# Reordering the VectorE and ScalarE queues of a graph attention kernel: V's low parts, softmax parts and squares

## The reference

```python
output = einsum('bni,io->bno', x, weight)
q, k   = x @ wq, x @ wk
alpha  = einsum('bno,bmo->bnm', q, k)
alpha  = maximum(alpha, 0.0) * (adj != 0)
alpha  = softmax(alpha, axis=1)
y      = x + einsum('bnm,bmo->bno', alpha, output)
out    = (y - mean(y)) / sqrt(var(y) + 1e-5)
```

## Time and profile before

| | before |
|---|---|
| median of 3 runs | 539.57 us (539.29 to 541.98) |
| the profiled execution, device time | 538.71 us |
| its span, first to last instruction | 536.9 us |
| granted TensorE clock | 0.997 |
| TensorE matmul busy | 515.9 us, 96% |
| VectorE busy | 386.4 us, 72% |
| ScalarE busy | 321.1 us, 60% |
| GpSimd busy | 267.2 us, 50% |
| one group, span 141.90 to 205.50 | 63.60 us, of which TensorE busy 62.13 us |

### The profile page before, as it was taken

One profiled execution on the slowest core, in us unless ns is written; L12 is line 12 of the kernel. 1 busy time (PEld: TensorE's weight loads), 2 busy tenths in 40 slices (PEclk: granted clock), 3 DMA queues, 4 the chain that ended last, 5 costly groups with the idle time before them and its releaser, 6 DMA issues.

```text
span 536.9 us, 9927 instructions
## 1 busy us (share of the span) xinstructions
PE 515.9 (96%) x3259; PEld 466.1 (87%) x3259; DVE 386.4 (72%) x741; ACT 321.1 (60%) x745; POOL 267.2 (50%) x198
## 2 busy tenths in 40 slices
PE   8999999999999999999999999999999999999993
PEld 6889997898979988799978989789897998879993
DVE  4767745779568786588857796577956978656676
ACT  5666565385853856648554676538585385664663
POOL 0397964358525567148551495435852565710002
PEclk9999999999999999999999999999999999999998
DMA  7405231053600625025240344205260062302344
GB/s 268 163 0 197 83 132 43 21 155 120 235 20 20 215 85 208 20 81 185 105 175 20 117 155 160 95 20 183 90 234 20 23 211 104 150 1 74 122 156 156
DMA packets 30719, 62.05 MB, mean 116 GB/s; under 512 B 2032, under 2 KB 3056, under 8 KB 30704
## 3 DMA queue, kind: packets, MB, share of 16 engines
q1 hardware_dynamic: 30704, 61.87, 33.3%
HBM read 45.09 MB, written 16.78 MB: 115 GB/s over the span
## 4 chain that ended last, share of the span: by engine, by line
PE 84%; DVE 9%; issue 3%; ACT 2%; DMA 1%; POOL 0%; DVEq 0%; POOLq 0%; SPq 0%; ACTq 0%
PE o_bank L293 11%; PE o_bank L295 11%; PE o_bank L294 11%; PE chain L293 10%; PE chain L295 9%; PE chain L294 9%; PE bank_y L293 5%; PE bank_y L294 5%; PE bank_y L295 5%; DVE p_lo L1052 3%; DVE v_lo L979 3%; PE bank_z L293 2%; PE bank_z L295 2%; PE bank_z L294 2%; DVE parts L991 1%
## 5 line engine op out<-in xcount | busy, mean ns | idle before, releaser
L1349 POOL TENSOR_TENSOR s_lo<-xs,s_hi 128x512 fp32r<-128x512 f32 x60 | 87.7, 1480 | 49.4 <-ACT s_hi L668 49.0
L1344 POOL TENSOR_TENSOR a_lo<-xt,a_hi 128x512 fp32r<-128x512 f32 x42 | 59.9, 1434 | 46.1 <-ACT a_hi L660 46.1
L1354 POOL TENSOR_TENSOR rstd<-var_eps,minus_half 128x4 f32<-128x4 f32 x15 | 15.3, 1018 | 117.1 <-DVE var_eps L1076 117.1
L295 PE MATMUL o_bank<-t_hi,a_lo 128*128 128x256 f32 x256 | 72.4, 283 | 0.0
L294 PE MATMUL o_bank<-t_lo,a_hi 128*128 128x256 f32 x256 | 72.4, 283 | 0.0
L293 PE MATMUL o_bank<-t_hi,a_hi 128*128 128x256 f32 x256 | 72.4, 283 | 0.0
L1052 DVE SCALAR_TENSOR_TENSOR p_lo<-soft,inv_sum,p_hi 128x256 fp32r<-128x256 f32 x64 | 55.2, 881 | 17.8 <-ACT p_hi L747 17.8
L1340 POOL TENSOR_TENSOR xs<-xt 128x512 f32<-128x512 f32 x30 | 39.6, 1336 | 41.8 <-DMA xt<-in_x_t 23.9
L687 ACT COPY parts<-chain 128x256 f32<-128x256 f32 x90 | 33.3, 371 | 42.6 <-PE chain L295 41.5
L677 ACT COPY parts<-chain 128x512 f32<-128x512 f32 x42 | 24.7, 587 | 47.1 <-DVE v_lo L979 32.0
L293 PE MATMUL o_bank<-v_hi,p_hi 128*128 128x512 f32 (+1 forms) x132 | 50.7, 384 | 1.4 <-DVE soft L1035 1.4
(11 more groups left out here) (191 smaller groups left out, 1599.0 us busy)
## 6 DMA issues: line engine op xcount, KB each, us to landing
xt<-in_x_t SPq DMA_DIRECT2D x64, 256.0 KB, 3.4
xn<-in_x SPq DMA_DIRECT2D x16, 1024.0 KB, 5.3
out<-xn SPq DMA_DIRECT2D x15, 1024.0 KB, 4.3
adj<-in_adj_t SPq DMA_DIRECT2D x16, 512.0 KB, 6.0
xn<-in_w SPq DMA_DIRECT2D x4, 256.0 KB, 4.6
xn<-in_wq_t SPq DMA_DIRECT2D x4, 256.0 KB, 6.0
parts<-in_wk_t SPq DMA_DIRECT2D x4, 256.0 KB, 6.1
out<-xn SPq DMA_DIRECT2D x4, 256.0 KB, 2.0
```

What stands on the lines that cost most here:

```text
L295: return nc.tensor.matmul(dst, a[1], b[0], start=False, stop=last, skip_group_check=shared)
L1344: nc.gpsimd.tensor_tensor(a_lo[:, slot, u], xt[:, u], a_hi[:, slot, u].bitcast(F32), ALU.subtract).then_inc(a_lo_ready[slot], 1)
L1349: nc.gpsimd.tensor_tensor(s_lo[:, slot, s], xs[:, s], s_hi[:, slot, s].bitcast(F32), ALU.subtract).then_inc(s_lo_ready[slot], 1)
```

## The change

All semaphore counts stay as they are; only the order of steps in ScalarE's and VectorE's lists changes. No step is added or removed.

- VectorE, start of a group: v_lo A22, v_lo A21 and p_lo 0 of z go ahead of T's first sum, p_lo 1 ahead of its second.
- ScalarE, start of a group: the first squares of y go from between two casts of V to just before copy_t(P6, 0), split_s(S2) stands ahead of v_hi A21, p_hi 1 and split_s(S4) ahead of copy_t(P1, 0), p_hi 3 ahead of copy_t(P6, 0).
- Both, pair a: each p part goes one or more steps ahead of V's parts; VectorE's p_lo 2 and 3 go ahead of mask(b, 0). ScalarE's casts for the next group's a (split_a, split_s) go behind p_hi 3.
- Last step: the four squares of pair 14 go between V's copies and splits on ScalarE; on VectorE its variance goes ahead of v_lo A12 and its first normalisation ahead of v_lo A21.

```diff
--- before.py
+++ after.py
@@ -762,20 +762,20 @@
                 a, b, z, y = 2 * i, 2 * i + 1, 2 * i - 1, 2 * i - 2
                 split_p(z, 0)
                 split_v(z, A22)
-                centred_squares(y, 0, 0)
+                split_s(i, 1, S2)
                 split_v(z, A21)
+                split_p(z, 1)
+                split_s(i, 1, S4)
                 copy_t(i, P1, 0)
-                split_s(i, 1, S2)
-                split_s(i, 1, S4)
                 copy_t(i, P1, 1)
                 split_s(i, 1, S1)
                 split_a(i, 1, A22)
-                split_p(z, 1)
                 split_p(z, 2)
+                split_p(z, 3)
+                centred_squares(y, 0, 0)
                 copy_t(i, P6, 0)
                 split_t_a(i, A11)
                 copy_t(i, P6, 1)
-                split_p(z, 3)
                 copy_t(i, P5, 0)
                 copy_t(i, P5, 1)
                 centred_squares(y, 0, 1)
@@ -799,30 +799,27 @@
                 exponent(a, 2)
                 copy_v(a, P6, 1)
                 exponent(a, 3)
+                split_p(a, 0)
                 copy_v(a, P5, 0)
                 copy_v(a, P5, 1)
-                split_p(a, 0)
-                if more:
-                    split_a(i + 1, 0, A21)
                 split_p(a, 1)
                 v_released(a)
                 split_v(a, A22)
+                split_p(a, 2)
+                split_v(a, A11)
+                split_p(a, 3)
                 if more:
+                    split_a(i + 1, 0, A21)
                     split_s(i + 1, 0, S2)
+                split_v(a, A12)
+                if more:
                     split_s(i + 1, 0, S3)
                     split_s(i + 1, 0, S1)
-                split_v(a, A11)
-                split_v(a, A12)
-                if more:
                     split_a(i + 1, 0, A11)
-                split_p(a, 2)
+                split_v(a, A21)
                 if more:
                     split_a(i + 1, 0, A12)
                     split_s(i + 1, 0, S4)
-                split_v(a, A21)
-                split_p(a, 3)
-
-                if more:
                     split_a(i + 1, 0, A22)
 
                 act.wait_ge(t_lo_ready, 8 * i + 4 + T_LO[1][A12])
@@ -851,24 +848,24 @@
                 for r in range(R):
                     exponent(p, r)
                 copy_v(p, P1, 0)
+                split_p(p, 0)
                 copy_v(p, P1, 1)
-                split_p(p, 0)
+                split_p(p, 1)
+                split_p(p, 2)
                 copy_v(p, P6, 0)
-                split_p(p, 1)
+                centred_squares(p - 1, 0, 0)
                 copy_v(p, P6, 1)
-                split_p(p, 2)
+                centred_squares(p - 1, 0, 1)
                 copy_v(p, P5, 0)
                 split_p(p, 3)
                 copy_v(p, P5, 1)
-                centred_squares(p - 1, 0, 0)
+                centred_squares(p - 1, 0, 2)
                 v_released(p)
                 split_v(p, A22)
-                centred_squares(p - 1, 0, 1)
+                centred_squares(p - 1, 0, 3)
                 split_v(p, A11)
                 split_v(p, A12)
-                centred_squares(p - 1, 0, 2)
                 split_v(p, A21)
-                centred_squares(p - 1, 0, 3)
                 for r in range(R):
                     centred_squares(p, 1, r, by_tile=True)
 
@@ -1086,13 +1083,13 @@
                 a, b, z, y = 2 * i, 2 * i + 1, 2 * i - 1, 2 * i - 2
                 split_v(z, A11, V_AT[1])
                 sum_v(z, A21)
+                split_v(z, A22, V_AT[1])
+                split_v(z, A21, V_AT[1])
+                split_p(z, 0)
                 sum_t(i, A11, 0)
-                split_v(z, A22, V_AT[1])
-                split_p(z, 0)
+                split_p(z, 1)
                 sum_t(i, A11, 1)
-                split_p(z, 1)
                 split_p(z, 2)
-                split_v(z, A21, V_AT[1])
                 split_p(z, 3)
                 sum_t(i, A22, 0)
                 sum_t(i, A22, 1)
@@ -1124,18 +1121,18 @@
                 split_t_b(i, A22)
                 split_t_b(i, A21)
                 invert(a)
+                split_p(a, 0)
                 sum_v(a, A22)
-                split_p(a, 0)
+                split_p(a, 1)
                 sum_v(a, A11)
                 split_v(a, A22, V_AT[0])
-                split_p(a, 1)
+                split_p(a, 2)
                 split_v(a, A11, V_AT[0])
+                split_p(a, 3)
                 split_v(a, A12, V_AT[0])
                 sum_v(a, A21)
 
                 mask(b, 0)
-                split_p(a, 2)
-                split_p(a, 3)
                 split_v(a, A21, V_AT[0])
                 mask(b, 1)
                 residual(a, i, 0, 0)
@@ -1308,11 +1305,12 @@
             sum_v(last, A11)
             split_v(last, A22, V_LAST)
             split_v(last, A11, V_LAST)
+            variances(last - 1)
             split_v(last, A12, V_LAST)
             sum_v(last, A21)
+            normalise(last - 1, 0, 0)
             split_v(last, A21, V_LAST)
-            variances(last - 1)
-            for r in range(R):
+            for r in range(1, R):
                 normalise(last - 1, 0, r)
             for r in range(R):
                 residual(last, GROUPS - 1, 1, r, bank=bank_y[:, 0] if r == R - 1 else None)
```

## The result

| | before | after |
|---|---|---|
| median | 539.43 us (538.47 to 541.98, 4 runs) | 524.39 us (523.67 to 526.05, 4 runs) |
| span of the profiled execution | 536.9 us | 522.0 us |
| first T matmul of group 1 | 77.62 us | 77.63 us |
| a group, first T matmul to first T matmul | 63.60 to 63.65 us | 61.64 us, all six |
| last residual chain, first residual to end of the last normalisation | 6.55 us | 6.55 us |

A forecast was written before the change was run, and what follows sets the result against it. TensorE, busy 515.9 of 536.9 us, was taken to bound the kernel. Gains of 10.3 + 2.8 + 1.7 = 14.8 us gave 523.9 from the profiled execution or 524.8 from the median; predicted 524.4 us, own range 523.0 to 526.5.

The forecast's parts named there:

- T gap: TensorE's wait at T's P5 for ScalarE's copy of P6, 1.48 us in each of seven groups, 10.3 us to gain.
- mask gap: TensorE's wait for VectorE's mask of b's second half, 0.47 us in each of six groups, 2.8 us to gain.
- last step: The last pair's first residual on VectorE starts earlier; gain 1.7 us, bounds 0.8 to 1.8.
- Change 1: V's last low parts go into VectorE's 4.40 us hole before T's first sum, freeing ScalarE's copy; gain 10.3 us.
- Rival B: T's first sum comes late, P2's second half starts 1.3 us late seven times; 533.5 us, chance 0.06.
- rival C: Another step still holds P6's copies at T's start, half of 10.3 us remains; 529.6 us, chance 0.05.
- Change 2: Softmax parts ahead of V's in pair a let VectorE's mask start earlier; gain 2.8 us.
- slip of the root: GpSimd's run starts later, so the root of z's variance behind it comes 1.1 to 2.1 us later.
- rival A: The late root makes TensorE wait 0.4 to 1.0 us for sum_v(b, A22) in six groups; 527 to 530.4 us, chance 0.15.
- cover: Slack between the root and P4 of pair b: 0.95 us idle before sum_v plus 0.78, together 1.73 us.
- rival D: GpSimd's eight steps take 1.81 us each, TensorE waits 3.8 us in six groups; 8 us slower, 547.6 us, chance 0.03.
- Change 3: In the last step, pair 14's squares, variance and one normalisation go earlier, advancing the last pair's first residual; gain 1.7 us.

The follow-up runs named there:

- e1: The kernel before with only v_lo A22 and v_lo A21 of z ahead of T's first sum on VectorE; 529.5 us.
- e2: The kernel before with only pair a's softmax parts ahead of V's parts on both engines, GpSimd's first cast behind p_hi 3; 535.81 us.
- e4: The kernel before with only p_hi 0 of pair a ahead of copy_v(P5, 0) and p_lo 0 ahead of sum_v A22; 536.13 us, one run.
- e3: The kernel before with only the last step changed: pair 14's squares, variance and one normalisation earlier; 537.4 us, ratio 0.997.
- e8: The changed kernel with p_lo 1 and p_lo 2 of z also ahead of T's two first sums on VectorE; 531.15 us, one run.
- e7: The changed kernel with three more roots on GpSimd ahead of the root of z in groups 1 to 6; 533.47 us, one run.
- e6: The changed kernel with one more root on GpSimd ahead of the root of z in groups 1 to 6; 526.5 us, one run.

## Why the prediction was right

**The sum held term by term, not only in total.**

| term | predicted us | measured us |
|---|---|---|
| T gap | 7 x 1.48 = 10.3 | 7 x 1.47 = 10.3 (e1: 63.60 - 62.14 = 1.46 a group) |
| mask gap | 6 x 0.47 = 2.8 | 6 x 0.48 = 2.9 (e2), of it 2.6 by p_lo 0 alone (e4) |
| last step | 1.7 | 1.60 (e3) |
| span | 522.1 | 522.0 |

The step that carried it was to take the gaps from the starts of matmuls, and not the slices of the page (the last of the forty shows TensorE busy for three tenths, where the prediction read nine or more in all but the first; nothing was added up from it). The listed waits say 8.6 + 1.4 = 10.0 us for the two gaps, the starts 13.1; the groups fell by 6 x 1.97, and with group 7's gap that is 13.3.

**Change 1.** The 0.34 us that ScalarE's copy of P6 should have to spare are 0.33. What I mis-sized is the work put in the hole: about 2.5 us expected, 3.3 measured (202.09 to 205.38). The two v_lo took 2.90 instead of 1.36, because GpSimd's sum and, one behind it, the s_lo whose cast the change moves forward fell on them; e1, which leaves that cast, has 1.79 for the same two. VectorE still had 1.19 us left. Rival B names the right place (e8) and did not happen, nor did rival C.

**Change 2.** "Nearly the whole 0.47 is won by this alone" is what e4 shows. The slip of the root was mis-sized: 1.1 to 2.1 us were expected. In before's time (this group stands 2.00 + 1.48 = 3.48 earlier at this place) GpSimd's run started at 182.81 and not at 183.4, took 10.7 us for eight subtractions instead of 11.0 to 12.05, and ended near 193.5, 1.1 us later than before and not about 2; the root came at 193.49, where it had been at 193.31: a slip of 0.2. The eight had taken 1.51 each with six of VectorE's instructions with two inputs in SBUF among them; four of these six now run before GpSimd starts, and it took 1.33. I had bounded it by the duration of a first instruction (1.37), which was itself stretched; 1.29 is the quiet one (188.77). The slip that I had put against the change was 1 to 2 us too long, and rival A was farther off than its condition said. Not in the forecast was that the steps between the root and sum_v(b, A22) would take 0.4 us more (6.38 us from 191.06 to 197.44, before 194.37 to 201.27 less 0.95 idle = 5.95; a_lo went from 0.69 to 1.44 beside GpSimd). Of the 1.73 us of cover, read with a handover of 0.24, 0.2 + 0.4 were used and 1.1 were left.

**Rivals A and D** name the right place: e7 shows the wait at P4. Their price was one for one beyond the cover, counted from the root. Counted from sum_v that holds (e6 and e7); counted from the root it was 0.34 for 1.0 us and 1.62 for 3.0 us, because the steps in between stretch and shrink. By e7's 1.62 us and one for one beyond it (this is argued, not run), the whole gain of 14.9 us would be lost at 2.5 us a group, with the root some 3.9 us later than in the changed kernel, which is 4.1 later than before; the prediction had said 4.2. The sum of rival D has an error: its slip of 5.5 us is counted from the end of GpSimd's run at 192.41 and not from the root at 193.31, where the other sums count from. It is 4.6, the wait 2.9 and the kernel 2.6 us slower, not 8.

**The handover.** The prediction took 0.24 us, read from a copy on ScalarE, for every step that releases TensorE. From the end of the step to the start of the matmul it is 0.24 for that copy, 0.15 for the mask on VectorE (before, six times) and 0.05 to 0.06 for VectorE's sums (e6, e7 and e8, nineteen times). The covers of the sums were 0.2 us larger than read, and the mask needed 0.1 less; the gains do not hang on it.

**Change 3.** 0.40 us, not 0.32, pass between the start of the last matmul and the residual, in e3 and in the changed kernel alike. The rest of the chain is 6.55 us in both kernels, as predicted.

The prediction took the middle between the profiled execution's base (523.9) and the median's (524.8); the median is 524.39.

## What to carry to other kernels

Where the bounding engine has few gaps, take each from the distance of its starts, multiply by how often it recurs, and look on the releasing engine's list for the step whose input had long been ready: two moved lines gave ten of the fifteen microseconds here, and moving one softmax part on two engines gave 2.6 more. Then read how much cover each step behind the move has, and take the time from a step's end to what it releases for that very pair of engines, and note that the cover is eaten at uneven speed: a short instruction that shifts beside another engine's long one can grow by more than the shift. Compare variants by the length of a repeated group, not by the span, when the start of the program varies by as much as the edits.

## What the runs showed of the hardware

**The start varies.** Over the thirteen profiled executions the first T matmul of group 1 came between 77.50 and 79.89 us, in code that none of the edits touched. For e1 the weight's load, shown above, accounts for 1.5 of its 2.27 us; for the others the cause stays open (e3 came at 78.25 with its first cast at 4.61). The groups behind it repeat within 0.05 us.

**A tiny VectorE instruction can wait for a whole GpSimd one.** The means, 128 x 4 values from and to SBUF, took 0.17 us at this place of the changed kernel and 1.24 beside GpSimd's s_lo in e6, 0.57 in e7, where they met its last part. In the groups 1 to 6 of the changed kernel the other means of a group took 1.07 to 1.23, each beside a sum of GpSimd's. Sums of 128 x 512 with one input in PSUM took 0.67 to 0.69 wherever they stood. The Trainium skill (SBUF — State Buffer, Who interferes with whom) says that VectorE and GpSimd share a port pair as an exclusive lock, taken by a VectorE instruction with two SBUF inputs and by forms of tensor_scalar, to which the means belong, and that one with at most one SBUF input outside those forms does not contend; these durations agree with it.
